# Softmax totals of two attention stages: inverted in their row by VectorE and spread over 64 partitions by one transfer

## The chip, the cores and the metric

The kernel runs on one core of a Trainium2 chip. The metric is the device time of one execution in microseconds (us). Three timed runs of the kernel before gave a median of 3260.16 us (3257.28 to 3265.87). One more execution was profiled; all rows shown here are from that one.

Engines are named as in the profile: PE is TensorE (matmuls), PEld its weight loads, DVE VectorE, ACT ScalarE, POOL GpSimd, SP the engine that only issues transfers.

## The reference

The program is four gated blocks, L0 to L3, each an attention and a feed-forward part, on x of 2 batches x 1024 tokens x 256. The change touches the attentions of L1 (4 heads) and L3 (16 heads); head size is 64, keys are 1024 tokens plus 154 context rows. Cut to what matters, for L3:

```python
dots = jnp.einsum('bhid,bhjd->bhij', q, k) * scale
attn = jax.nn.softmax(dots, axis=-1)
out = jnp.einsum('bhij,bhjd->bhid', attn, v)
return out @ Wo + bo
```

The division of the softmax is done last: a row of ones rides along with v, so that the product gives 64 rows of output and a 65th row with the totals, and the output is multiplied by the inverse of the totals.

## The kernel before, in words

Both stages run the same functions, in **units** of one pair of heads and one batch: L1 has 4 units, L3 has 16. A unit has 40 **slots**; in each, a chunk of up to 128 keys meets a block of 512 queries. Ten slots make one **group** (one head, one block of 512 queries), so a unit has four groups, 0 to 3. In a slot PE multiplies keys with queries (L1978, L1979), ACT takes the exponential (L2022, L2023), in L3 DVE subtracts the rounded high part to get a low part, `pt_lo` (L2129), and PE multiplies with v a few slots later (L1968): `lag` is 4 slots in L3 and 2 in L1, where there is no `pt_lo` and PE takes slots two at a time.

The order on each engine is written out by hand, and each engine works through its list in order. Around the slots a unit also prepares the next one:

- In slots 2 to 11 (L3) PE projects q, k and v of the next unit; ACT rounds them; DVE makes the low parts (L2087, L2075). They go through two side banks in turn, so PE may write a part only when the part two before it was read. In L1 DVE makes low parts in slots 2 to 6 (L2540), and PE's first score waits for all of them (`lo_kept`).
- In slots 8 to 36 PE computes 16 **scores** of the next unit (L1919), one every second slot (two in slots 22, 23 and 24), into one set of three banks. DVE takes the row maximum of each, a `TENSOR_REDUCE` over 1178 columns (L2103). PE may not begin a score before the maximum of the score before it is taken (`maxed`, L1912).
- After the 8th and the 16th score PE transposes the maxima (L1883), in slots 24 and 38, and DVE writes their negatives into the queries (L2066). PE does not begin the next unit before both side banks are read (L1952).
- In slots 14 to 35 PE multiplies scaled outputs with the output weights (L1891) and DVE adds them to x (L2095).

The end of a group runs through four engines. `keep_group` (ACT, L2037) copies 65 rows from the bank into `a.out`, in slot 4 (L3) or 2 (L1) of the next group. SP (`move_totals`) moves the row of totals, 512 numbers in one partition, onto 128 partitions x 4 (`a.totals`, L2138). DVE (`invert_group`) takes the reciprocal there (L2148). SP moves it back into a row (L2141) and waits for it. POOL (`scale_group`) spreads the row over 64 partitions (L2157, a custom instruction) and multiplies (L2161); `ot_done` counts that. ACT waits for `ot_done` of the group two before it ahead of overwriting `a.out`; PE waits for it ahead of the products with the output weights (L1891; for the last unit L1897). DVE inverts a group 7 (L3) or 6 (L1) slots after its end, and group 3 in slot 12 of the next unit. `attention_end` does the last group of the stage. There are 65 inversions in L3 and 17 in L1 (one of each for a dummy group).

The rows of the trace call `a.totals` `l3a_totals` and `l1a_totals`, and so on; in L1 `out_t` is a part of `chip_xn`, and k2 and q2 show as `l3a_k` and `l3a_q`.

Of the kernel before, what the change touches and what calls it, by code (L numbers as in the profile page):

```python
# [19 lines left out]
P = 128  # L20
# [1746 lines left out]
class Attention:  # L1767
# [4 lines left out]
    def __init__(self, sb, psum, sem, projected, gate, split=False, out_t=None):  # L1772
        self.gate, self.split = gate, split
        self.lag = 4 if split else 2
        self.slots_together = 1 if split else 2
        self.pt_slots = 5 if split else 4
        self.exp_slots = 4
        self.prepares = 8 if split else 7
        self.q1 = sb("q1", [P, 2, 2, SEQ], F32R)
        self.q2 = sb("q2", [P, 2, 2, SEQ], F32R)  # L1780
        self.k1 = sb("k1", [P, 2, 2, KEYS], F32R)
        self.k2 = sb("k2", [P, 2, 2, KEYS], F32R)
        self.v = sb("v", [P, 2, KEY_CHUNKS, 2, HEAD + 1], F32R if split else F32)
        self.pt = sb("pt", [P, 4, BLOCK])
        if split:
            self.v_lo = sb("v_lo", [P, 2, KEY_CHUNKS, 2, HEAD + 1], F32R)
            self.pt_hi, self.pt_lo = sb("pt_hi", [P, self.pt_slots, BLOCK], F32R), sb("pt_lo", [P, self.pt_slots, BLOCK], F32R)
            self.v_kept, self.lo_made = sem("v_kept"), sem("lo_made")
        self.maxima = sb("maxima", [P, 16])
        self.minus = sb("minus", [8, 8])  # L1790
        self.out = sb("out", [P, 2, BLOCK])
        self.totals = sb("totals", [P, BLOCK // P])
        self.inverse = sb("inverse", [1, BLOCK])
        self.shared = sb("shared", [P, BLOCK])
        self.out_t = sb("out_t", [P, 2, SEQ]) if out_t is None else out_t
        self.banks = banks = psum("banks", [P, 6, 512])
        self.s_bank, self.st_bank, self.o_bank = banks[:, 0:3, :], banks[:, 3:5, :], banks[:, 5, :]
        self.first_banks = (banks[:, 0:3, :], banks[:, 3:6, :])
        self.side = psum("side", [P, 2, 512])
        self.side_read = [sem("side_read0"), sem("side_read1")]  # L1800
        self.prepared, self.side_done, self.hi_kept = sem("prepared"), sem("side_done"), sem("hi_kept")
        self.q_doubled, self.k_doubled = sem("q_doubled"), sem("k_doubled")
        self.scored, self.maxed, self.st_done, self.exped = sem("scored"), sem("maxed"), sem("st_done"), sem("exped")
        self.pv_done, self.o_kept, self.moved = sem("pv_done"), sem("o_kept"), sem("moved")
        self.inverted, self.returned, self.row_returned = sem("inverted"), sem("returned"), sem("row_returned")
        self.spread_done, self.ot_done, self.passed = sem("spread_done"), sem("ot_done"), sem("passed")
# [326 lines left out]

def move_totals(sp, a, k, g):
    sp.wait_ge(a.o_kept, k + 1)
    sp.dma_start(a.totals[:], a.out[HEAD:HEAD + 1, g % 2, :]).then_inc(a.moved, 16)  # L2138
# [24 lines left out]


# [98 lines left out]
def l1_attention(nc, chip, I):  # L2263
# [7 lines left out]
    with ExitStack() as kept_stack:  # L2271
        sb, _, sem = scope(nc, kept_stack, "l1a")
# [9 lines left out]
        with ExitStack() as stack:  # L2282
            sb, psum, sem = scope(nc, stack, "l1p")
# [216 lines left out]
        with ExitStack() as stack:  # L2500
            sb, psum, sem = scope(nc, stack, "l1a2")
            a = Attention(sb, psum, sem, projected=False, gate=chip.gates[:, 1:2],
                                  out_t=chip.xn[:, 0:8, :].rearrange("p (u t) d -> p u (t d)", u=2))
# [94 lines left out]
def l3_attention(nc, chip, I):  # L2598
# [3 lines left out]
    with ExitStack() as stack:  # L2602
        sb, psum, sem = scope(nc, stack, "l3a")
# [4 lines left out]
        a = Attention(sb, psum, sem, projected=True, gate=chip.gates[:, 3:4], split=True)  # L2608
# [630 lines left out]
```

## Time and profile before

| | us |
|---|---|
| median of three timed runs | 3260.16 |
| the profiled execution: its time | 3260.37 |
| the profiled execution: its span | 3258.7 |
| PE busy in the span | 2897.2 (89%) |
| DVE busy | 1895.9 (58%) |
| ACT busy | 1430.0 (44%) |
| POOL busy | 660.4 (20%) |

The span is from the first to the last instruction; 1.7 us lie around it. Busy shares are means over stages with different limits. L1's attention runs from about 400 to 747 us of the span, L3's from about 1600 to 2862 us. In a timeline a row gives start, duration, engine, line, operation, what it writes from what, and in brackets the idle time ahead of it and what ended it; "issue" means that the profile shows nothing that it waited for.

### The profile page before, as it was taken

How to read it: one execution, taken by the hardware profiler on the slowest of the kernel's cores; microseconds unless marked ns; L12 is line 12 of the kernel's file. 1: busy time of each engine (PE TensorE's matmuls, PEld its weight loads, DVE VectorE, ACT ScalarE, POOL GpSimd, SP SyncE). 2: the span in 40 equal slices, each digit the busy share in tenths (PEclk: the TensorE clock that was granted, in tenths of full speed). 3: DMA queues.
4: the chain of work that ended last, by engine and by line, in shares of the span. 5: the costliest groups of instructions: out<-in, count | busy, mean ns of one | idle time of the engine just before them, and what ended most of it. 6: DMA issues, size and time to landing. Idle time of an engine off the chain costs nothing. (4 is left out here: it accounts for less than half of the span.)

```text
span 3258.7 us, 46897 instructions
## 1 busy us (share of the span) xinstructions
PE 2897.2 (89%) x14020; PEld 2132.3 (65%) x14021; DVE 1895.9 (58%) x3602; ACT 1430.0 (44%) x2987; POOL 660.4 (20%) x736
## 2 busy tenths in 40 slices
PE   6795789975998889999689999999999999579997
PEld 4795455535886679999556666666666666345664
DVE  4414464405555454443588888888888888363333
ACT  1232634431221114544447777767666777321111
POOL 0133101111442200000201111111111111106776
PEclk8797889995999879999789999999999999879999
DMA  1342000002332010000000001010000000035776
GB/s 39 122 148 86 9 20 15 15 1 91 102 103 79 15 40 27 26 13 1 24 21 17 23 15 33 19 23 15 23 21 17 23 15 17 1 70 151 163 163 140
DMA packets 147165, 158.11 MB, mean 49 GB/s; under 512 B 36816, under 2 KB 121702, under 8 KB 146726
## 3 DMA queue, kind: packets, MB, share of 16 engines
q1 hardware_dynamic: 109318, 94.41, 10.5%
q0 software_dynamic: 21280, 37.93, 5.3%
q10 hardware_dynamic: 16416, 24.12, 2.2%
q8 instruction: 50, 0.82, 0.1%
q14 instruction: 101, 0.83, 0.1%
HBM read 105.77 MB, written 29.84 MB: 42 GB/s over the span
## 5 line engine op out<-in xcount | busy, mean ns | idle before, releaser
L2022 ACT ACTIVATE l3a_pt_hi<-l3a_banks 128x512 fp32r<-128x512 f32 (+2 forms) x640 | 382.0, 597 | 322.2 <-PE l3a_banks L1968 255.0
L2129 DVE TENSOR_TENSOR l3a_pt_lo<-l3a_pt,l3a_pt_hi 128x512 fp32r<-128x512 f32 (+2 forms) x640 | 464.0, 730 | 95.5 <-ACT l3a_pt L2023 91.3
L2023 ACT ACTIVATE l3a_pt<-l3a_banks 128x512 f32<-128x512 f32 (+2 forms) x640 | 378.1, 591 | 0.0
L2103 DVE TENSOR_REDUCE l3a_maxima<-l3a_banks 128x1 f32<-128x1178 f32 x256 | 351.1, 1374 | 3.0 <-PE l3a_banks L1919 1.4
L1968 PE MATMUL l3a_banks<-l3a_pt_hi,l3a_v 128*65 128x512 f32 (+2 forms) x640 | 286.4, 447 | 8.1 <-ACT l3a_out L2037 7.3
L1978 PE MATMUL l3a_banks<-l3a_q,l3a_k 128*128 128x512 f32 (+2 forms) x640 | 257.2, 402 | 7.7 <-DVE l3a_q L2066 5.0
L1979 PE MATMUL l3a_banks<-l3a_q,l3a_k 72*128 72x512 f32 (+5 forms) x640 | 254.1, 397 | 0.0
L1968 PE MATMUL l3a_banks<-l3a_pt_hi,l3a_v_lo 128*65 128x512 f32 (+2 forms) x640 | 252.6, 395 | 0.0
L1968 PE MATMUL l3a_banks<-l3a_pt_lo,l3a_v 128*65 128x512 f32 (+2 forms) x640 | 252.6, 395 | 0.0
L1919 PE MATMUL l3a_banks<-l3a_k,l3a_q 128*128 128x512 f32 (+1 forms) x768 | 216.8, 392 | 16.7 <-DVE l3a_maxima L2103 15.4
L2157 POOL PARTITION_BROADCAST l3a_shared<-l3a_inverse x65 | 62.1, 955 | 624.2 <-issue 624.2
L2161 POOL TENSOR_TENSOR l3a_out_t<-l3a_out,l3a_shared 64x512 f32<-64x512 f32 x65 | 88.8, 1366 | 470.5 <-issue 470.5
L1919 PEld LDWEIGHTS l3a_banks<-l3a_k,l3a_q 128*128 128x128 f32 x768 | 142.5, 196 | 62.2 <-DVE l3a_maxima L2103 39.4
L1978 PEld LDWEIGHTS l3a_banks<-l3a_q,l3a_k 128*128 128x128 f32 (+2 forms) x640 | 115.8, 181 | 78.6 <-issue 14.8
L2913 POOL DMA_INDIRECT l3f_sums<-l3f_y_rows,l3f_token_index x96 | 147.8, 1540 | 53.9 <-DVE l3f_row_weight L3176 31.5
L1610 ACT ACTIVATE l2f_hidden_hi<-l2f_p_h,l2f_b_pair 128x512 fp32r<-128x512 f32 x128 | 89.2, 697 | 151.1 <-PE l2f_p_h L1563 140.1
L1968 PE MATMUL l1a_banks<-l1a_pt,l1a_v 128*65 128x512 f32 (+2 forms) x320 | 152.5, 599 | 1.7 <-ACT l1a_out L2037 1.7
L1662 DVE TENSOR_TENSOR l2f_hidden_lo<-l2f_hidden,l2f_hidden_hi 128x512 fp32r<-128x512 f32 x128 | 88.6, 692 | 107.6 <-ACT l2f_hidden L1611 107.6
L1002 PE MATMUL l1f_p_h<-l1f_xt_tile,l1f_w 128*128 128x128 f32 x1184 | 142.3, 279 | 7.1 <-issue 6.1
L1002 PEld LDWEIGHTS l1f_p_h<-l1f_xt_tile,l1f_w 128*128 128x128 f32 x1184 | 138.0, 195 | 14.5 <-issue 14.3
L3009 PE MATMUL l3f_p_h<-l3f_xt,l3f_w 128*128 128x320 f32 x512 | 144.7, 436 | 1.1 <-DVE l3f_xt L3169 1.1
L1577 PE MATMUL l2f_p_y<-l2f_w_hi,l2f_hidden_lo 128*128 128x256 f32 x512 | 144.7, 283 | 0.0
(584 smaller groups left out, 6060.0 us busy)
## 6 DMA issues: line engine op xcount, KB each, us to landing
l3f_w<-in_L_ffn_w SPq DMA_DIRECT2D x96, 256.0 KB, 3.7
l0f_w<-in_L_ffn_W ACTq DMA_DIRECT2D x12, 1024.0 KB, 6.5
l1f_w<-in_L_ffn_W ACTq DMA_DIRECT2D x18, 512.0 KB, 5.1
l2f_w<-in_L_ffn_w SPq DMA_DIRECT2D x16, 512.0 KB, 4.3
l3a_q<-l3a_q SPq DMA_DIRECT2D x64, 128.0 KB, 2.3
l3a_k<-l3a_k SPq DMA_DIRECT2D x64, 128.0 KB, 2.3
l0f_w<-in_L_ffn_W SPq DMA_DIRECT2D x4, 1024.0 KB, 7.2
l1f_w<-in_L_ffn_W SPq DMA_DIRECT2D x6, 512.0 KB, 8.5
```

The costliest lines, as they stand in the source:

```text
L1002: ins = pe.matmul(p_h[:, bank, (f % 2) * P:(f % 2 + 1) * P], w[:, u, c, f * P:(f + 1) * P], xt_tile[:, c * P:(c + 1) * P], start=c == 0, s ...
L1577: ins = pe.matmul(p_y[:, bank, half * D:(half + 1) * D], h[:, n % 2, f, j * P:(j + 1) * P], a[:, u, 1, f * D:(f + 1) * D], start=f == 0 an ...
L1919: ins = pe.matmul(banks[:, c, 0:end - at], lhs, a.k1[:, u, h, at:end], start=True, stop=not masked)
L1968: ins = pe.matmul(a.o_bank[0:HEAD + 1, :], v[0:rows, u, c, h, :], pt[0:rows, slot, :], start=c == 0 and k == 0, stop=c == KEY_CHUNKS - 1 a ...
L1978: pe.matmul(a.st_bank[0:rows, n % 2, :], a.k1[:, u, h, row:row + rows], a.q1[:, u, h, queries], start=True, stop=False)
L1979: pe.matmul(a.st_bank[0:rows, n % 2, :], a.k2[second, u, h, row:row + rows], a.q2[second, u, h, queries], start=False, stop=True).then_inc ...
L2022: act.activation(a.pt_hi[0:rows, n % a.pt_slots, :], a.st_bank[0:rows, n % 2, :], ACT.Exp, bias=bias, scale=scale)
L2023: act.activation(a.pt[0:rows, n % 4, :], a.st_bank[0:rows, n % 2, :], ACT.Exp, bias=bias, scale=scale).then_inc(a.exped, 1)
L2103: dve.tensor_reduce(a.maxima[:, n:n + 1], banks.rearrange("p a b -> p (a b)")[:, 0:KEYS], AX.X, ALU.max).then_inc(a.maxed, 1)
L2129: dve.tensor_tensor(a.pt_lo[0:rows, slot, :], a.pt[0:rows, n % 4, :], a.pt_hi[0:rows, slot, :].bitcast(F32), ALU.subtract).then_inc(a.lo_m ...
L2913: pool.indirect_dma_start(sums, bass.IndirectOffsetOnAxis(token_index[0:n, u, j:j + 1], 0), y_rows[0:n, u, j, :], None, compute_op=ALU.add ...
L3009: ins = pe.matmul(p_h[:, k + f, 0:CAP], w[:, u, c, f * P:(f + 1) * P], xt[:, u, c, :], start=c == 0, stop=c == DC - 1)
```

## The change

`a.totals`, `a.inverse` and the two transfers through them are gone. DVE waits for ACT's copy and takes the reciprocal of the totals in place, in row 64 of `a.out`: 512 numbers in one partition, where it was 4 numbers in each of 128. One transfer, issued by SP, copies that row onto 64 partitions of `a.shared`, which now has two buffers. POOL only multiplies. The inversion stands in slot `lag + 1` of the next group: 5 slots after a group's end in L3, 3 in L1, for group 3 too (slot 5 or 3 of the next unit).

```diff
-        if n == 12:
+        if n == a.lag + 1:
             invert_group(dve, a, number(unit, -1), 3)
-        if n > 10 and n % 10 == (7 if a.split else 6):
+        if n > 10 and n % 10 == a.lag + 1:
             invert_group(dve, a, number(unit, n // 10 - 1), n // 10 - 1)
...
-def move_totals(sp, a, k, g):
-    sp.wait_ge(a.o_kept, k + 1)
-    sp.dma_start(a.totals[:], a.out[HEAD:HEAD + 1, g % 2, :]).then_inc(a.moved, 16)
+def spread_inverse(sp, a, k, g):
+
     sp.wait_ge(a.inverted, k + 1)
-    sp.wait_ge(a.spread_done, k + 1)
-    sp.dma_start(a.inverse[:], a.totals[:]).then_inc(a.returned, 16)
-    sp.wait_ge(a.returned, k * 16 + 16)
-    sp.sem_inc(a.row_returned, 1)
+    sp.dma_start(a.shared[:, g % 2, :], a.out[HEAD:HEAD + 1, g % 2, :].unsqueeze(1).to_broadcast([1, HEAD, BLOCK])).then_inc(a.spread_out[g % 2], 16)
 
 
 def invert_group(dve, a, k, g):
-    dve.wait_ge(a.moved, k * 16 + 16)
-    dve.reciprocal(a.totals[:], a.totals[:]).then_inc(a.inverted, 1)
+
+    dve.wait_ge(a.o_kept, k + 1)
+    totals = a.out[HEAD:HEAD + 1, g % 2, :]
+    dve.reciprocal(totals, totals).then_inc(a.inverted, 1)
...
     pool.wait_ge(a.ot_done, k + 2)
-    pool.wait_ge(a.returned, k * 16 + 16)
     pool.sem_inc(a.passed, 1)
-    pool.partition_broadcast(a.shared[0:HEAD, :], a.inverse[:], channels=HEAD).then_inc(a.spread_done, 1)
-    pool.wait_ge(a.spread_done, k + 2)
-    pool.sem_inc(a.passed, 1)
+    pool.wait_ge(a.spread_out[g % 2], k * 8 + (8 + 8 * (g % 2)))
```

On DVE, in the loop of L3, slots 14 to 16 of a unit before (`l3a_maxima` is the row maximum of a score, `l3a_pt_lo` the slot's low part; REGISTER_ALU and ISA rows are bookkeeping and waits):

```order
L2103 TENSOR_REDUCE l3a_maxima<-l3a_banks 128x1
L2128 REGISTER_ALU
L2129 TENSOR_TENSOR l3a_pt_lo<-l3a_pt,l3a_pt_hi 128x512
L2128 REGISTER_ALU
L2129 TENSOR_TENSOR l3a_pt_lo<-l3a_pt,l3a_pt_hi 128x512
L2094 REGISTER_ALU
L2095 SCALAR_TENSOR_TENSOR chip_x<-l3a_side,chip_gates,chip_x 128x256
L2102 REGISTER_ALU
L2103 TENSOR_REDUCE l3a_maxima<-l3a_banks 128x1
```

The same slots now:

```order
L2101 TENSOR_REDUCE l3a_maxima<-l3a_banks 128x1
L2126 REGISTER_ALU
L2127 TENSOR_TENSOR l3a_pt_lo<-l3a_pt,l3a_pt_hi 128x512
L2142 REGISTER_ALU
L2144 RECIPROCAL l3a_out<-l3a_out 1x512
L2126 REGISTER_ALU
L2127 TENSOR_TENSOR l3a_pt_lo<-l3a_pt,l3a_pt_hi 128x512
L2092 REGISTER_ALU
L2093 SCALAR_TENSOR_TENSOR chip_x<-l3a_side,chip_gates,chip_x 128x256
L2100 REGISTER_ALU
L2101 TENSOR_REDUCE l3a_maxima<-l3a_banks 128x1
```

The reciprocal of group 0 came behind the maximum of slot 16, with 4 columns; it now stands ahead of it, with 512.

On DVE, slots 4 and 5 of a unit in the same loop before (`l3a_k` the low part of the next unit's keys):

```order
L2087 TENSOR_TENSOR l3a_k<-l3a_side,l3a_k 64x512 x2
L2128 REGISTER_ALU
L2129 TENSOR_TENSOR l3a_pt_lo<-l3a_pt,l3a_pt_hi 128x512
L2082 REGISTER_ALU
L2087 TENSOR_TENSOR l3a_k<-l3a_side,l3a_k 64x512 x2
```

And now:

```order
L2085 TENSOR_TENSOR l3a_k<-l3a_side,l3a_k 64x512 x2
L2126 REGISTER_ALU
L2127 TENSOR_TENSOR l3a_pt_lo<-l3a_pt,l3a_pt_hi 128x512
L2142 ISA
L2144 RECIPROCAL l3a_out<-l3a_out 1x512
L2080 REGISTER_ALU
L2085 TENSOR_TENSOR l3a_k<-l3a_side,l3a_k 64x512 x2
```

The reciprocal of the last unit's group 3 has moved here from slot 12, between the two halves of the keys.

On POOL, one group in the same loop before:

```order
L2154 REGISTER_ALU
L2155 ISA
L2157 ISA
L2157 ISA l3a_shared<-l3a_inverse 64x512
L2161 ISA
L2161 TENSOR_TENSOR l3a_out_t<-l3a_out,l3a_shared 64x512
```

And two groups now:

```order
L2152 ISA
L2154 TENSOR_TENSOR l3a_out_t<-l3a_out,l3a_shared 64x512
L2150 REGISTER_ALU
L2152 ISA
L2154 TENSOR_TENSOR l3a_out_t<-l3a_out,l3a_shared 64x512
```

The custom instruction (the ISA row that writes `l3a_shared`) is gone, and with it one ISA row ahead of it and one behind it that had no other line of the program than L2157 and L2161.

## Rows read from the trace of the kernel before

**Rows 1.** Busy us per engine (PE, PEld, DVE, ACT, POOL), granted clock; L3's middle
```profile
1690.00:2760.00 1070.00, 1050.32 (x4759) 726.00 (x4757) 919.32 (x1314) 757.33 (x1518) 137.32 (x118) 1.00 0.09 20
```

**Rows 2.** Single lines: reciprocals on DVE, ns min/median/max, first and last start
```profile
L2148 DVE RECIPROCAL l3a_totals<-l3a_totals x65: 162/169/178, 1685.0 to 2836.5; 128x4 f32<-128x4 f32 x65
...
L3090 DVE RECIPROCAL l3f_total<-l3f_total x1: 253/253/253, 2890.4 to 2890.4; 128x16 f32<-128x16 f32 x1
```

**Rows 3.** Timeline, L3, one unit, slots 15 to 18: DVE, and PE's next score
```profile
2202.47 0.69 DVE L2129 TENSOR_TENSOR l3a_pt_lo<-l3a_pt,l3a_pt_hi 128x512 fp32r<-128x512 f32 x1 [0.35 <-ACT l3a_pt L2023]
...
2203.48 1.37 DVE L2103 TENSOR_REDUCE l3a_maxima<-l3a_banks 128x1 f32<-128x1178 f32 x1
...
2205.78 0.89 PE L1919 MATMUL l3a_banks<-l3a_k,l3a_q 128*128 128x512 f32 x3
```

**Rows 4.** Timeline, the same unit, slots 26 to 28
```profile
2220.98 1.38 DVE L2103 TENSOR_REDUCE l3a_maxima<-l3a_banks 128x1 f32<-128x1178 f32 x1
...
2223.14 0.89 PE L1919 MATMUL l3a_banks<-l3a_k,l3a_q 128*128 128x512 f32 x3
```

**Rows 5.** Timeline, the same unit, slot 38 and PE's start of the next unit
```profile
2239.81 1.21 DVE L2066 TENSOR_TENSOR l3a_q<-l3a_side,l3a_minus 8x1024 fp32r<-8x1024 f32 x1
...
2241.26 0.49 PE L1978 MATMUL l3a_banks<-l3a_q,l3a_k 128*128 128x512 f32 x1 [0.20 <-DVE l3a_q L2066]
```

**Rows 6.** Timeline, the next unit, slot 5 on DVE and slot 7 on PE
```profile
2255.94 1.39 DVE L2087 TENSOR_TENSOR l3a_k<-l3a_side,l3a_k 64x512 fp32r<-64x512 f32 x2 [0.77 <-ACT l3a_k L2057]
...
2257.38 1.16 PE L2635 MATMUL l3a_side<-l3a_w,chip_xt 128*128 128x128 f32 x8
```

**Rows 7.** Timeline, L1, one unit, slots 3 to 8 and 12 to 14
```profile
517.23 1.39 DVE L2540 TENSOR_TENSOR l1a_q<-chip_xt,l1a_q 64x512 fp32r<-64x512 f32 x2 [0.52 <-ACT l1a_q L2521]
...
519.13 4.47 DVE L2540 TENSOR_TENSOR l1a_k<-l1a_k_t,l1a_k 64x512 fp32r<-64x512 f32 x6 [0.52 <-ACT l1a_k L2521]
...
523.65 0.81 PE L1919 MATMUL l1a_banks<-l1a_k,l1a_q 128*128 128x512 f32 x3
...
530.37 0.70 PE L1919 MATMUL l1a_banks<-l1a_k,l1a_q 128*128 128x512 f32 x3
...
531.22 1.38 DVE L2103 TENSOR_REDUCE l1a_maxima<-l1a_banks 128x1 f32<-128x1178 f32 x1 [1.71 <-PE l1a_banks L1921]
...
533.90 0.89 PE L1919 MATMUL l1a_banks<-l1a_k,l1a_q 128*128 128x512 f32 x3
```

**Rows 8.** Transfers by line: issues, KB each, median us to landing
```profile
l3a_q<-l3a_q SPq DMA_DIRECT2D x64, 128.0 KB, 2.3
```

**Rows 9.** Timeline, POOL, one group near the end of L3
```profile
2813.08 0.80 POOL L2157 PARTITION_BROADCAST l3a_shared<-l3a_inverse  x1 [6.14 <-issue]
...
2821.39 1.25 POOL L2161 TENSOR_TENSOR l3a_out_t<-l3a_out,l3a_shared 64x512 f32<-64x512 f32 x1 [7.50 <-issue]
```

**Rows 10.** End of L1: a row of the waits (us, times, longest), then timeline
```profile
PE l1a_side L1897 <- POOL chip_xn L2161: 26.0, 2, 21.6
...
721.05 0.58 ACT L2037 COPY l1a_out<-l1a_banks 65x512 f32<-65x512 f32 x1 [3.45 <-PE l1a_banks L1968]
...
742.57 3.84 PE L1897 MATMUL l1a_side<-l1a_wo,chip_xn 128*128 128x256 f32 x8 [21.55 <-POOL chip_xn L2161]
```

**Rows 11.** L3's last unit and end: two rows of the waits, then timeline
```profile
PE l3a_side L1897 <- issue: 36.0, 2, 23.6
...
PE l3a_banks L1968 <- ACT l3a_out L2037: 7.3, 3, 3.5
...
2833.90 0.58 ACT L2037 COPY l3a_out<-l3a_banks 65x512 f32<-65x512 f32 x1 [2.77 <-PE l3a_banks L1968]
```

**Rows 12.** L3: a wait in another unit, then windows behind it and behind 2775.8
```profile
2434.62 1.07 PE L1919 MATMUL l3a_banks<-l3a_k,l3a_q 128*128 128x512 f32 x3 [1.55 <-DVE l3a_maxima L2103]
...
2434.20:2437.60 3.40, 2.98 (x8) 1.98 (x9) 2.83 (x4) 0.04 (x1) 0.00 (x0) 0.61 0.00 0
...
2775.80:2779.20 3.40, 3.37 (x9) 2.32 (x10) 0.90 (x2) 1.95 (x4) 0.00 (x0) 0.57 0.04 5
```

More of the change, by code:

```diff
@@ L1791, in __init__ @@
         self.out = sb("out", [P, 2, BLOCK])
-        self.totals = sb("totals", [P, BLOCK // P])
-        self.inverse = sb("inverse", [1, BLOCK])
-        self.shared = sb("shared", [P, BLOCK])
+        self.shared = sb("shared", [HEAD, 2, BLOCK])
         self.out_t = sb("out_t", [P, 2, SEQ]) if out_t is None else out_t
@@ L1803, in __init__ @@
         self.scored, self.maxed, self.st_done, self.exped = sem("scored"), sem("maxed"), sem("st_done"), sem("exped")
-        self.pv_done, self.o_kept, self.moved = sem("pv_done"), sem("o_kept"), sem("moved")
-        self.inverted, self.returned, self.row_returned = sem("inverted"), sem("returned"), sem("row_returned")
-        self.spread_done, self.ot_done, self.passed = sem("spread_done"), sem("ot_done"), sem("passed")
+        self.pv_done, self.o_kept = sem("pv_done"), sem("o_kept")
+        self.inverted, self.ot_done, self.passed = sem("inverted"), sem("ot_done"), sem("passed")
+        self.spread_out = [sem("spread_out0"), sem("spread_out1")]
         self.parts = Q_PARTS + V_PARTS if projected else ()
@@ L2130, in attention_dve @@
                               ALU.subtract).then_inc(a.lo_made, 1)
-def move_totals(sp, a, k, g):
-    sp.wait_ge(a.o_kept, k + 1)
-    sp.dma_start(a.totals[:], a.out[HEAD:HEAD + 1, g % 2, :]).then_inc(a.moved, 16)
+def spread_inverse(sp, a, k, g):
     sp.wait_ge(a.inverted, k + 1)
-    sp.wait_ge(a.spread_done, k + 1)
-    sp.dma_start(a.inverse[:], a.totals[:]).then_inc(a.returned, 16)
-    sp.wait_ge(a.returned, k * 16 + 16)
-    sp.sem_inc(a.row_returned, 1)
+    sp.dma_start(a.shared[:, g % 2, :], a.out[HEAD:HEAD + 1, g % 2, :].unsqueeze(1).to_broadcast([1, HEAD, BLOCK])).then_inc(a.spread_out[g % 2], 16)
 def invert_group(dve, a, k, g):
-    dve.wait_ge(a.moved, k * 16 + 16)
-    dve.reciprocal(a.totals[:], a.totals[:]).then_inc(a.inverted, 1)
+    dve.wait_ge(a.o_kept, k + 1)
+    totals = a.out[HEAD:HEAD + 1, g % 2, :]
+    dve.reciprocal(totals, totals).then_inc(a.inverted, 1)
 def scale_group(pool, a, k, g, parity):
     pool.wait_ge(a.ot_done, k + 2)
-    pool.wait_ge(a.returned, k * 16 + 16)
     pool.sem_inc(a.passed, 1)
-    pool.partition_broadcast(a.shared[0:HEAD, :], a.inverse[:], channels=HEAD).then_inc(a.spread_done, 1)
-    pool.wait_ge(a.spread_done, k + 2)
-    pool.sem_inc(a.passed, 1)
+    pool.wait_ge(a.spread_out[g % 2], k * 8 + (8 + 8 * (g % 2)))
     b, (hi, _) = g // 2, head_rows(g % 2)
-    pool.tensor_tensor(a.out_t[hi, parity, b * BLOCK:(b + 1) * BLOCK], a.out[0:HEAD, g % 2, :], a.shared[0:HEAD, :],
+    pool.tensor_tensor(a.out_t[hi, parity, b * BLOCK:(b + 1) * BLOCK], a.out[0:HEAD, g % 2, :], a.shared[:, g % 2, :],
                        ALU.mult).then_inc(a.ot_done, 1)
@@ L2174, in attention_sync @@
         double_parts(sp, a, unit + 1, 1 - u)
-    move_totals(sp, a, number(unit, -1), 3)
-    move_totals(sp, a, number(unit, 0), 0)
+    spread_inverse(sp, a, number(unit, -1), 3)
+    spread_inverse(sp, a, number(unit, 0), 0)
     if extra is not None:
         extra("v4")
-    move_totals(sp, a, number(unit, 1), 1)
+    spread_inverse(sp, a, number(unit, 1), 1)
     if extra is not None:
         extra("o7")
-    move_totals(sp, a, number(unit, 2), 2)
+    spread_inverse(sp, a, number(unit, 2), 2)
 def attention_start_act(act, chip, a):
@@ L2197, in attention_end @@
     if sp is not None:
-        move_totals(sp, a, k, 3)
+        spread_inverse(sp, a, k, 3)
     if dve is not None:
@@ L2583, in _ @@
                 pool.wait_ge(a.prepared, a.prepares)
-                pool.sem_inc(a.spread_done, 1)
                 pool.sem_inc(a.ot_done, 2)
@@ L2739, in _ @@
             pool.wait_ge(a.prepared, a.prepares)
-            pool.sem_inc(a.spread_done, 1)
             pool.sem_inc(a.ot_done, 2)
```

## The prediction

> **What bounds the kernel now.** I read the page first (which engine is busy in which slice), then the windows over the two attentions, then the timeline slot by slot, and the waits at both ends. In the middle of L3 PE is busy 1050.3 of 1070 us at a clock of 1.00, so PE sets the pace; the reader should look at DVE beside it, busy 919.3, or 86% [rows 1]. From the first and the last start of its reciprocals, 64 groups take 1151.5 us, so a unit of four takes 72.0 us [rows 2], and DVE's idle time in it is 14%, 10.1 us. It is not spread so that a long instruction finds room: a gap is such as the 0.35 us in slot 15 [rows 3], and PE's next score waits for DVE's last row maximum. Both stages end otherwise: PE stands still for POOL. At the end of L1 two waits make 26.0 us [rows 10]; in L3's last unit PE waits 36.0 us for the scaled groups and 7.3 us for ACT, which cannot overwrite `a.out` before POOL has read it [rows 11].
>
> **POOL's part.** A group's two POOL instructions take 0.80 and 1.25 us, but 6.1 us lie ahead of the first and 7.5 us ahead of the second, in which POOL waits for nothing that the profile shows [rows 9]. The order shows an extra row ahead of each; they go with the custom instruction. So a group costs POOL 15.7 us before and about 1.3 us after. Within the stage this hides behind PE; at the ends it does not.
>
> **The new reciprocal.** The trace has none with 512 columns. Four columns take 169 ns, 16 take 253 [rows 2]: 7.0 ns for each further column, so 0.169 + 508 x 0.007 = 3.7 us. That 1 partition replaces 128 does not help: a DVE instruction on 8 partitions takes 1.21 us for 1024 columns [rows 5], no less per column than the maximum on 128, 1.37 us for 1178 [rows 3]. From below, 512 columns cannot cost less than a `pt_lo` of 512, 0.69 us [rows 3]; from above, 253 ns for 16 taken as a rate gives 8.1 us. I take the slope. DVE starts an instruction about 0.1 us before the one ahead ends, so it is held for D = 3.6 us.
>
> The Trainium skill, "VectorE: DVE Perf Modes", under "First, the fixed hardware budget", says that the reciprocal divides iteratively, with a repeat count of 8. Eight steps of about 1.04 ns for each of 512 columns would be 4.4 us with a base of 0.1, an estimate by that page; the rows' slope is under seven such steps, and the measured slope decides here.
>
> **What D displaces in L3.** DVE works in order, so everything behind the reciprocal is late by D less the gap it fills.
>
> - Slot 15: the gap of 0.35 is filled, and the maximum of slot 16, which ended at 2204.85, ends D - 0.35 later; PE's score at 2205.78 needs it [rows 3]. PE stands for D - 0.35 - 0.93 = D - 1.3.
> - Slot 25: the maximum that ended at 2222.36 ends D later, the score is due at 2223.14 [rows 4]: D - 0.8.
> - Slot 35: the negated maxima at 2239.81 come D later, less 0.1 for the old reciprocal, and PE opens the next unit 0.2 us after them, waiting already [rows 5]: D - 0.1.
> - Slot 5: the keys' low part comes D - 0.77 late and ended 0.05 us before PE reuses its bank [rows 6]: D - 0.8.
>
> Together 4D - 3.0 = 11.4 us in each of the 15 units that prepare a next one: 171 us. The last unit has no scores; its low parts may be nearly four slots late. Between 0 and 4 x 3.6 us, I take 4.
>
> PE's stops can also cost clock. In one unit the maximum came late, PE stood 1.55 us, and the granted clock over the next 3.4 us was 0.61, most of it 1.2 GHz instead of 2.4; behind the longest wait of the last unit, 3.5 us [rows 11], it was 0.57 [rows 12]. Such a fall costs (1 - 0.6) x 3.4 = 1.4 us. How often it follows a stop two rows cannot tell. I take one fall for three stops: 0.5 us for each of 60, 30 us.
>
> **What D displaces in L1.** DVE has no `pt_lo` here. Slot 3: it takes the place of two gaps of 0.52, and PE's first score begins 0.05 us after the last low part [rows 7]: D - 1.1 = 2.5. Slot 13: it starts as the maximum of slot 12 ends, at 532.5; with 0.4 taken for one addition to x in between and 1.4 for the next maximum DVE is done at 537.9, while a score 3.53 us after that at 533.90 would be due at 537.4: 0.5. Slot 33 likewise; slot 23 stands between two scores of one slot pair, I take 1.5. Three units by 5.0 us: 15 us.
>
> **What the ends give back.** The path after the change is ACT's copy 0.58, reciprocal 3.7, transfer, POOL 1.25 and 0.2 of handing over. The transfer has 64 rows of 2 KB; the q halves are the same size between partitions and land in 2.3 us [rows 8]. That all 64 reads come from one partition no row shows: 2.3 is the lower end, three times it, 6.9, my upper one, which would take 2 x 4.6 = 9 us from the return. That makes 8.0 us from the start of the copy, which begins as PE stops: of L1's 26.0 us of waits 8.1 are left, with PE's next matmul at 729.1 instead of 742.57, and 17.9 come back [rows 10]; in L3 8.1 are left of 36.0 + 7.3, and 35.2 come back [rows 11]. About 3 us more come from falls of the clock that no longer follow the earlier waits, two at 1.4.
>
> **At no cost.** SP issues one transfer for two and no longer waits for one to return; a reader behind it in the queue gains. DVE's new wait for ACT's copy finds it done: the copy stands one slot earlier, and in L3 DVE has already waited for the exponential behind it. If that cover were gone, it is the 0.58 us of the copy.
>
> **Sum**, against the profiled time 3260.4 (the median of the runs shown is 3260.2): + 171 + 4 + 30 (L3) + 15 (L1) - 17.9 - 35.2 - 3 = 3424, rounded 3425 us.
>
> **The rivals.**
>
> - *The idle time takes it (0.16).* If low parts, side banks and scores let DVE run at 100%, only what exceeds its idle time counts: 4 x 3.6 - 10.1 = 4.3 us a unit, 65 in L3, with about 10 in L1 and 56 back: 3280. For it speaks that several buffers lie between the engines; against it that the scores have one set of banks, and PE already waits for a late maximum now and then [rows 12].
> - *The reciprocal is short (0.10), faster.* At 0.69 us, D is 0.6; only slot 35 still delays, 0.5 x 15 = 8, and the ends give 56: 3212. The point that decides is D = 1.6, where slots 5, 15, 25 and 35 cost 0.8, 0.3, 0.8 and 1.5 us, 51 in L3, about what the ends return. Against it stands the slope between 4 and 16 columns; for it, that no row shows 512.
> - *A longer division (0.14).* As a mechanism of these rows: 7.0 ns is a slope between two short instructions, and the shorter may hide part of its steps behind its start, so that the slope is steeper further out, D 4.3 instead of 3.6. Each 0.1 us of D costs 60 x 0.1 in L3 and 12 x 0.1 in L1; 0.7 us more give 50 and 3475. (By the Trainium skill, "VectorE: DVE Perf Modes", the section named above, its estimate is where this rival lies; no row here shows it.)
> - *Every stop costs clock (0.08).* If each of the 60 stops is followed by 3.4 us at half speed, about 1.4 us are lost instead of 0.5, 54 more: 3480. [...]
>
> **Numbers.** The forecast as reckoned has 0.50, its own range 3360 to 3465; 0.02 is left for what I did not think of. The range that should hold 8 in 10 runs from 3275 to 3490: it takes in the longer division, most of the absorbed case and part of the lost clock, and leaves out the short reciprocal. A difference under 0.3%, 10 us, cannot be told from none. Slower holds the forecast, the longer division, the lost clock and most of the absorbed case, 0.86; within 0.3% part of the absorbed case, 0.04; faster 0.10.
>
> **What the new profile would show.** Right: the reciprocal of 1x512 at 3.6 to 4.4 us; in L3's middle units of about 85 us, DVE busy over 90%, PE under 90%, and PE's scores (L1919) waiting for the maxima some 2 to 3 us after slots 15 and 25, and its start of a unit for the negated maxima; POOL with 1.3 us and no gaps of 6 to 7; PE's last wait in each stage about 8 us. Wrong: a reciprocal near 1 us; or a full-length one with units still near 76 us, which means that the buffers took it; or a transfer that lands after 5 us or more.

## The result, and the profile after

The changed kernel takes 3404.67 us (median of 4 runs, 3401.42 to 3411.74), against 3261.28 for the kernel before beside it: a ratio of 1.0442, 95% interval 1.0423 to 1.0462. It is 143 us slower; the prediction was 3425, in a range of 3275 to 3490. The profiled execution took 3411.74 us, 151.4 more than the profiled one of before; the parts below add up to that.

The page and the transfers of the kernel after (busy us, share, instructions; then KB and us from issue to landing):

```profile
PE 2954.8 (87%) x14020; PEld 2155.9 (63%) x14021; DVE 2151.2 (63%) x3602; ACT 1431.8 (42%) x2987; POOL 579.1 (17%) x654
...
L2144 DVE RECIPROCAL l3a_out<-l3a_out 1x512 f32<-1x512 f32 x65 | 217.4, 3344 | 4.7 <-ACT l3a_out L2035 2.7
...
l3a_shared<-l3a_out SPq DMA_DIRECT2D x65, 128.0 KB, 6.3
```

The reciprocal takes 3.34 us and the transfer 6.3. PE has as many instructions as before, but is busy 57.6 us longer: that is clock. One unit in the middle of L3, from the reciprocal of a group 0 to that of the next unit's group 0 (windows, columns as in [rows 1]), first of the kernel before and then of the kernel after:

```profile
2205.36:2278.06 72.70, 71.78 (x328) 49.67 (x327) 64.10 (x92) 51.90 (x105) 9.02 (x9) 1.00 0.08 16
```

```profile
2198.50:2284.00 85.50, 75.52 (x327) 51.14 (x327) 75.11 (x91) 51.63 (x105) 5.13 (x4) 0.96 0.26 28
```

The same work of PE takes 85.5 us. Of the 12.8 us more, 9.1 are idle time of PE (9.98 instead of 0.92) and 3.7 are longer busy time at a clock of 0.96 instead of 1.00. Over 14 units, from one reciprocal of group 3 to the next, a unit takes 85.7 us (1662.48 to 2861.86) and took 73.2 (1684.96 to 2709.52).

PE's waits for DVE in that unit (timeline of PE, kernel after); slot 15's reciprocal started at 2198.47, the others at 2218.93, 2238.51 and 2261.70:

```profile
2204.28 0.81 PE L1917 MATMUL l3a_banks<-l3a_k,l3a_q 128*128 128x512 f32 x3 [1.84 <-DVE l3a_maxima L2101]
...
2212.81 0.81 PE L1917 MATMUL l3a_banks<-l3a_k,l3a_q 128*128 128x512 f32 x3 [0.37 <-DVE l3a_maxima L2101]
...
2215.09 0.80 PE L1917 MATMUL l3a_banks<-l3a_k,l3a_q 128*128 128x512 f32 x3 [0.21 <-DVE l3a_maxima L2101]
...
2224.34 1.35 PE L1917 MATMUL l3a_banks<-l3a_k,l3a_q 128*128 128x512 f32 x3 [2.43 <-DVE l3a_maxima L2101]
...
2243.93 0.27 PE L1881 MATMUL l3a_side<-chip_ident,l3a_maxima 128*8 128x128 f32 x1 [2.34 <-DVE l3a_maxima L2101]
...
2266.52 1.16 PE L2627 MATMUL l3a_side<-l3a_w,chip_xt 128*128 128x128 f32 x8 [2.52 <-DVE l3a_k L2085]
```

Each of the four reciprocals is followed by a stop of 1.8 to 2.5 us. Over the whole run PE waits for DVE in three places more than before (total us, times, longest), first the kernel before:

```profile
PE l3a_banks L1919 <- DVE l3a_maxima L2103: 15.4, 40, 1.6
...
PE l3a_side L1883 <- DVE l3a_maxima L2103: 3.1, 2, 1.6
```

And after, where the wait for the keys' low part has come in with slot 5:

```profile
PE l3a_banks L1917 <- DVE l3a_maxima L2101: 77.6, 73, 2.5
...
PE l3a_side L2627 <- DVE l3a_k L2085: 38.9, 16, 2.5
PE l3a_side L1881 <- DVE l3a_maxima L2101: 38.5, 17, 2.4
```

The granted clock over the 3.4 us behind each stop (windows of PE, kernel after, in the order of slots 15, 25, 35 and 5; PE busy, clock, DMA share, GB/s):

```profile
2204.28:2207.68 3.40, 3.40 (x16) 1.00 0.79 47
2224.34:2227.74 3.40, 3.40 (x9) 0.54 0.77 25
2243.93:2247.33 3.40, 3.40 (x10) 0.59 0.77 27
...
2266.52:2269.92 3.40, 3.40 (x23) 1.00 0.96 31
```

Two of the four are followed by a stretch mostly at 1.2 GHz. The longest stop, that of slot 5, is not, so its length alone does not decide it. Over the 15 units a stretch at the lower clock follows 14 stops of slot 25, 14 of slot 35, 3 of slot 5 and 1 of slot 15: 32 of 60.

The end of L1 in the kernel after (timeline), to be read beside [rows 10]:

```profile
728.30 0.58 ACT L2035 COPY l1a_out<-l1a_banks 65x512 f32<-65x512 f32 x1 [3.46 <-PE l1a_banks L1966]
...
728.91 3.35 DVE L2144 RECIPROCAL l1a_out<-l1a_out 1x512 f32<-1x512 f32 x1 [3.56 <-ACT l1a_out L2035]
...
732.28 0.46 SPq L2137 DMA_DIRECT2D l1a_shared<-l1a_out  x1
...
738.63 1.26 POOL L2154 TENSOR_TENSOR chip_xn<-l1a_out,l1a_shared 64x512 f32<-64x512 f32 x1 [12.53 <-DMA l1a_shared<-l1a_out]
...
740.03 1.19 PE L1895 MATMUL l1a_side<-l1a_wo,chip_xn 128*128 128x256 f32 x2 [11.77 <-POOL chip_xn L2154]
```

One wait of 11.8 us is left of 26.0. The end of L3 looks the same, 11.7 us left of 43.3 [rows 11]. The path is a copy, a reciprocal, a transfer of 6.3 us and a multiplication, and POOL waits for nothing but the transfer.

### The profile page after: what moved, and what is told of

It is laid out like the page before. It is cut to its first block and busy times, and to the rows that moved or that the text cites. A ratio compares the mean times of both kernels' runs of the same rounds, so it can differ in the third digit from the quotient of the medians.

```text
span 3410.0 us, 46109 instructions
## 1 busy us (share of the span) xinstructions
PE 2954.8 (87%) x14020; PEld 2155.9 (63%) x14021; DVE 2151.2 (63%) x3602; ACT 1431.8 (42%) x2987; POOL 579.1 (17%) x654
## 5 line engine op out<-in xcount | busy, mean ns | idle before, releaser
L2127 DVE TENSOR_TENSOR l3a_pt_lo<-l3a_pt,l3a_pt_hi 128x512 fp32r<-128x512 f32 (+2 forms) x640 | 454.6, 722 | 81.1 <-ACT l3a_pt L2021 76.2
L1966 PE MATMUL l3a_banks<-l3a_pt_hi,l3a_v 128*65 128x512 f32 (+2 forms) x640 | 294.9, 461 | 2.4 <-DVE l3a_pt_lo L2127 2.0
L1917 PE MATMUL l3a_banks<-l3a_k,l3a_q 128*128 128x512 f32 (+1 forms) x768 | 221.1, 399 | 78.8 <-DVE l3a_maxima L2101 77.6
L1976 PE MATMUL l3a_banks<-l3a_q,l3a_k 128*128 128x512 f32 (+2 forms) x640 | 265.0, 414 | 3.8 <-DVE l3a_q L2064 2.0
L1977 PE MATMUL l3a_banks<-l3a_q,l3a_k 72*128 72x512 f32 (+5 forms) x640 | 262.9, 411 | 0.0
L1966 PE MATMUL l3a_banks<-l3a_pt_lo,l3a_v 128*65 128x512 f32 (+2 forms) x640 | 261.2, 408 | 0.0
L1966 PE MATMUL l3a_banks<-l3a_pt_hi,l3a_v_lo 128*65 128x512 f32 (+2 forms) x640 | 260.1, 406 | 0.0
L1917 PEld LDWEIGHTS l3a_banks<-l3a_k,l3a_q 128*128 128x128 f32 x768 | 144.1, 201 | 135.6 <-DVE l3a_maxima L2101 114.3
L2144 DVE RECIPROCAL l3a_out<-l3a_out 1x512 f32<-1x512 f32 x65 | 217.4, 3344 | 4.7 <-ACT l3a_out L2035 2.7
L1976 PEld LDWEIGHTS l3a_banks<-l3a_q,l3a_k 128*128 128x128 f32 (+2 forms) x640 | 119.6, 187 | 72.8 <-issue 10.8
```

Of the source, the lines that this page charges most:

```text
L1917: ins = pe.matmul(banks[:, c, 0:end - at], lhs, a.k1[:, u, h, at:end], start=True, stop=not masked)
L1966: ins = pe.matmul(a.o_bank[0:HEAD + 1, :], v[0:rows, u, c, h, :], pt[0:rows, slot, :], start=c == 0 and k == 0, stop=c == KEY_CHUNKS - 1 a ...
L1976: pe.matmul(a.st_bank[0:rows, n % 2, :], a.k1[:, u, h, row:row + rows], a.q1[:, u, h, queries], start=True, stop=False)
L1977: pe.matmul(a.st_bank[0:rows, n % 2, :], a.k2[second, u, h, row:row + rows], a.q2[second, u, h, queries], start=False, stop=True).then_inc ...
L2144: dve.reciprocal(totals, totals).then_inc(a.inverted, 1)
```

## The experiments

The kernel before ran beside each group of runs; ratios are to it. Where totals stay undivided or outputs are zero, the routing of the later feed-forward stages changes a little too (13894 to 14020 matmuls), so stages are compared there, by the first and last start of L3's reciprocals: 1151.5 us apart before [rows 2], 1329.9 after the change.

**1 and 2. How the time goes with the length of the reciprocal.**

```diff
-    totals = a.out[HEAD:HEAD + 1, g % 2, :]
+    totals = a.out[HEAD:HEAD + 1, g % 2, 0:4]              # e1_short
+    totals = a.out[HEAD:HEAD + 1, g % 2, 0:BLOCK // 2]     # e2_half
```

> The changed kernel, but the reciprocal takes only the first 4 of a group's 512 totals (the other 508 stay undivided); transfer, place and POOL's part are those of the change. Theory (the length of the reciprocal on DVE delays row maxima and low parts, and PE stops for them): D falls from 3.3 to about 0.1 us, PE's stops of some 10 us a unit go, only the ends' return is left. Ends: 26.0 and 43.3 us of waits before become about 8.5 each, with 3 of clock: 3261 - 17.5 - 34.8 - 3 = 3206, range 3200 to 3225, faster than the kernel before. Rival (the transfer of one partition's row, 6.3 us and on every unit, is what costs): the transfer is the same, so the time stays at 3390 to 3405. Rival (the earlier slot costs): the slot is the same, 3390 to 3405 too.

> The changed kernel, but the reciprocal takes 256 of the 512 totals (the rest stays undivided). 0.17 + 252 x 0.0062 = 1.74 us. Theory with its four thresholds (stops of D - 0.8, D - 1.3, D - 0.8, D - 0.1 in slots 5, 15, 25, 35): 0.9 + 0.4 + 0.9 + 1.6 = 3.8 us of stops a unit instead of about 10, 57 us in 15 units and some 13 of clock; L1 about 2; ends give back 49 and 3: 3261 + 57 + 13 + 2 - 52 = 3281, range 3260 to 3305. Rival (idle time takes a short instruction up, and only what exceeds DVE's 10 us a unit counts): 4 x 1.74 is under 10, so no stop, 3210 to 3220. Rival (a cost that grows evenly with the columns, without thresholds): midway between the time with 4 columns and the 3405 with 512, about 3305 to 3310.

Four columns: 3212.23 us, ratio 0.985 (0.983 to 0.9871). Half: 3268.31, 1.0021 (1.0008 to 1.0035). The reciprocals of L3 with 4 columns (ns min/median/max, first and last start):

```profile
L2144 DVE RECIPROCAL l3a_out<-l3a_out x65: 168/169/172, 1652.6 to 2802.0; 1x4 f32<-1x4 f32 x65
```

And with half:

```profile
L2144 DVE RECIPROCAL l3a_out<-l3a_out x65: 1743/1744/1746, 1644.7 to 2852.2; 1x256 f32<-1x256 f32 x65
```

First to last start is 1149.4 us with 4 columns, 1207.5 with 256 and 1329.9 with 512. Transfer, slots and POOL's part are the same in all three, so neither the slow transfer nor the earlier slot is the loss: it is the reciprocal's length. The first 256 columns cost 56 us of run time, the next 256 136. So the cost does not grow evenly, as the thresholds of the four stops say, and idle time does not simply take the short one up.

**3. The same division in four pieces.**

```diff
-    dve.reciprocal(totals, totals).then_inc(a.inverted, 1)
+    totals = a.out[HEAD:HEAD + 1, g % 2, piece * P:(piece + 1) * P]
+    ins = dve.reciprocal(totals, totals)      # pieces 0 to 3 in slots lag + 1 to lag + 4
+    if piece == 3:
+        ins.then_inc(a.inverted, 1)
```

> The changed kernel, but each reciprocal of 512 columns is taken as four of 128 columns, about 0.95 us each, in four slots one after the other (slots 5 to 8 of the next group in L3, 3 to 6 in L1); the result is the same. DVE's work rises a little, 4 x 0.95 = 3.8 us a group instead of 3.34. Theory (the length of one hold counts, since gaps and buffers between the engines take a short one): most of the loss goes; DVE's total of some 76 us a unit against 72 is then the bound, 4 to 8 us a unit, 65 to 120 in L3, and 46 come back at the ends: 3280 to 3335. Rival (DVE's total time counts, not the length of a hold): 3405 + 15 x 4 x 0.4 = about 3430, not under 3400.

3387.42 us, 1.0397 (1.0375 to 1.0419): the theory's number failed. PE's waits for DVE (total us, times, longest):

```profile
PE l3a_banks L1917 <- DVE l3a_maxima L2101: 87.6, 102, 1.7
PE l3a_banks L1976 <- DVE l3a_q L2064: 41.6, 16, 2.7
...
PE l3a_side L1881 <- DVE l3a_maxima L2101: 18.2, 17, 1.6
```

No single hold is over 0.95 us, yet the three rows still make 147 us; 77.6, 38.9 and 38.5 make 155 in the changed kernel. What the pieces saved is mostly clock: PE is busy 2926.2 us. The trace of the kernel before tells why there was no gap for them. DVE's idle stretches from the first slot of a unit to slot 37 (timeline of DVE, kernel before; the idle time stands in brackets):

```profile
2171.09 1.00 DVE L2129 TENSOR_TENSOR l3a_pt_lo<-l3a_pt,l3a_pt_hi 128x512 fp32r<-128x512 f32 x1 [2.06 <-ACT l3a_pt L2023]
2173.11 0.69 DVE L2129 TENSOR_TENSOR l3a_pt_lo<-l3a_pt,l3a_pt_hi 128x512 fp32r<-128x512 f32 x1 [1.02 <-ACT l3a_pt L2023]
2175.15 1.39 DVE L2087 TENSOR_TENSOR l3a_q<-l3a_side,l3a_q 64x512 fp32r<-64x512 f32 x2 [1.34 <-ACT l3a_q L2057]
...
2199.15 0.69 DVE L2129 TENSOR_TENSOR l3a_pt_lo<-l3a_pt,l3a_pt_hi 128x512 fp32r<-128x512 f32 x1 [0.34 <-ACT l3a_pt L2023]
...
2226.37 0.69 DVE L2129 TENSOR_TENSOR l3a_pt_lo<-l3a_pt,l3a_pt_hi 76x512 fp32r<-76x512 f32 x1 [0.32 <-ACT l3a_pt L2023]
```

The lines left out hold 1.8 us in slots 3 to 6 and 1.2 in slots 10 and 11, and from 2198 to 2240 there are five more like the last two. So 7.3 of these 9.4 us lie ahead of slot 12, and from there to slot 37, where three of the four reciprocals stand, DVE had 2.05 us. The theory has to say: what counts in such a stretch is DVE's sum, not how long one hold is. In slot 5, where DVE has idle time of its own, the pieces do help: PE's wait there falls from 38.9 to 2.2 us.

**4. The old inversion, without POOL's custom instruction.** The 128x4 reciprocal and its two transfers as before, in the old slots; a third transfer spreads the row over 64 partitions.

```diff
+    sp.wait_ge(a.o_kept, k + 1)
+    sp.dma_start(a.totals[:], a.out[HEAD:HEAD + 1, g % 2, :]).then_inc(a.moved, 16)
     sp.wait_ge(a.inverted, k + 1)
+    sp.dma_start(a.inverse[:, g % 2, :], a.totals[:]).then_inc(a.returned, 16)
+    sp.wait_ge(a.returned, k * 16 + 16)
-    sp.dma_start(a.shared[:, g % 2, :], a.out[HEAD:HEAD + 1, g % 2, :]...
+    sp.dma_start(a.shared[:, g % 2, :], a.inverse[:, g % 2, :]...
```

> The changed kernel with the inversion of the kernel before: the totals go to 128 partitions x 4 by one transfer, the reciprocal of 128x4 stands in the slots of before, the inverses return into a row by a second transfer, and a third spreads the row over 64 partitions, so that POOL has no custom instruction. Theory (the loss is DVE's long reciprocal, the gain is POOL's custom instruction): stages run as in the kernel before, and at an end the path is copy 0.6 + transfer 2.1 + reciprocal 0.2 + transfer 2.1 + spreading transfer 6.3 + POOL 1.3 + 0.4 = 13 us instead of 26.0 in L1 and 43.3 in L3: 3261 - 13 - 30 - 3 = 3215, range 3205 to 3230, faster than both kernels. Rival (three transfers a group in SP's queue collide with the doubling of q and k, or the transfer of 6.3 us delays the last products): no gain, 3250 to 3300.

3228.78 us, 0.9911 (0.9892 to 0.9931), faster than both. The ends came as expected, 12.5 and 12.4 us. That it is not 3215 goes in part with waits that the kernel before has less of (PE waited 1.9 us in all for ACT's `l3a_pt` there):

```profile
PE l3a_banks L1979 <- ACT l3a_pt L2024: 10.5, 11, 1.8
```

and DVE waits 11.4 us for `l3a_totals` instead of 4.6. The rival names three transfers in one queue. Run 9 has three as well, and there these waits are back at 2.9 and 4.6 us: they go with how long the transfers take, the third above all (6.3 us here, 3.5 there), and not with their number.

**5 and 6. The place.**

```diff
+        if n == 12:                                            # e5_late: the slots of before
+        if n > 10 and n % 10 == (7 if a.split else 6):
...
+        if n == (39 if a.split else 33):                       # e6_slot39: group 2 alone
+            invert_group(dve, a, number(unit, 2), 2)
```

> The changed kernel with the reciprocal (512 columns in one partition) back in the slots of before: 7, 7 and 7 slots after a group's end in L3, 6 in L1, and slot 12 for group 3. Theory (DVE's time in a stretch where it has next to none to spare, wherever it stands there): the stops move by two slots, three of four stay as long; slot 12 stands among the first scores and is as bad as slot 5. 3390 to 3420, POOL's last group unmoved. Rival (the earlier slot is what costs): near 3230 to 3300.

> The changed kernel with one of the four reciprocals of an L3 unit moved: that of group 2 goes from slot 35, ahead of the last score's maximum and the negated maxima, to slot 39, behind them, where DVE has its gaps in the trace of before (2.1, 1.0 and 1.3 us in slots 38 to 1). Theory (a reciprocal costs nothing where DVE has idle time of its own): the stops of the transposition of the maxima, 38.5 us over the run, go, and some 8 us of clock with them: 3358, range 3345 to 3375; the other three stay. Rival (DVE's total counts, at whatever place): 3395 to 3410.

The old slots: 3440.7 us, 1.0535 (1.0502 to 1.0569), slower than expected: 36 us more than with the earlier ones. Its waits:

```profile
PE l3a_banks L1917 <- DVE l3a_maxima L2101: 105.9, 87, 2.5
PE l3a_banks L1976 <- DVE l3a_q L2064: 50.9, 16, 3.3
```

Three now stand among the scores, and slot 37's falls whole on the negated maxima (3.3 us a unit). PE is busy 2981.6 us, 27 more than after the change. So the move to earlier slots was a help, not a cost.

Slot 39: 3352.86 us, 1.0277 (1.0251 to 1.0303), as expected; the other two rows of waits stay, and the transposition's is gone:

```profile
PE l3a_banks L1917 <- DVE l3a_maxima L2101: 76.9, 69, 2.5
PE l3a_side L2629 <- DVE l3a_k L2085: 39.0, 16, 2.6
```

A reciprocal in DVE's own idle time adds no stop: 52 us come back, 27 of them as PE's busy time (2927.5).

**7 and 10. Less work for DVE elsewhere, alone and with the pieces.**

```diff
-... banks.rearrange("p a b -> p (a b)")[:, 0:KEYS], AX.X, ALU.max)
+... banks.rearrange("p a b -> p (a b)")[:, 0:KEYS // 2], AX.X, ALU.max)
```

> The changed kernel with each row maximum taken over 589 of the 1178 keys (a softmax is the same with any shift, so the output is too): 0.69 us less for each of 16 maxima, 11 us less DVE work a unit between slots 8 and 38, the reciprocals as they are. If DVE's sum over that stretch counts, the 11 us make up for three reciprocals (10 us): the stops for maxima (77.6 and 38.5 us) nearly vanish and only slot 5's stop, 38.9, stays: 3260 to 3290. If the length of one hold counts, since DVE cannot work ahead of PE's scores, only the one maximum behind each reciprocal is 0.69 shorter: stops of 1.3, 1.8 and 2.4 us stay beside the 2.5 of slot 5, some 37 us and 8 of clock less: 3360, range 3340 to 3375.

> Both edits together: the reciprocal in four pieces of 128 columns in four slots, and each row maximum over 589 keys. Each alone left 3387 and 3295. DVE's work in a unit is then 62 + 15 - 11 = 66 us of 72. If what counts is DVE's sum where it has no time to spare, and, once it has some, how long a single hold is, the two together leave few stops: 3215 to 3245. If the length of a hold plays no part at all, the pieces bring nothing on top: 3290 to 3305.

Alone: 3295.02 us, 1.0101 (1.0077 to 1.0125), far from the 3360 of the hold and just past the range of the sum:

```profile
PE l3a_side L2627 <- DVE l3a_k L2085: 38.5, 16, 2.5
PE l3a_banks L1917 <- DVE l3a_maxima L2101: 28.2, 36, 1.1
PE l3a_side L1881 <- DVE l3a_maxima L2101: 19.0, 17, 1.2
```

The stops for maxima fall from 116 to 47 us, none is over 1.2, and slot 5's is untouched, since no maximum stands ahead of it. Some 14 of the 110 us gained are L1's, which the expectation left out: its attention, whose maxima are halved too, takes 407.6 us from its first matmul to its last and 421.6 in the kernel after. The clock behind slot 5's stop shows that its place does not settle the matter either. Two of its 15 stops of 2.5 us (windows of PE, columns as above):

```profile
1720.90:1724.30 3.40, 3.40 (x23) 1.00 0.96 31
1798.82:1802.22 3.40, 3.40 (x13) 0.54 0.96 31
```

In the kernel after, 3 of 15 were followed by the lower clock; here 9 are, and 9 in run 6 too.

With the pieces too: 3274.91 us, 1.006 (1.0033 to 1.0087), between the two ranges. Slot 5's stop is gone (3.4 us in all), so the length of a hold does play a part there, but the last piece of group 2 stands in slot 38 ahead of the negated maxima, which the expectation overlooked:

```profile
PE l3a_banks L1976 <- DVE l3a_q L2064: 41.6, 16, 2.7
PE l3a_banks L1917 <- DVE l3a_maxima L2101: 24.2, 36, 1.1
```

**8, 11 and 12. The transfer by itself, and POOL's part.**

```diff
-a.out[HEAD:HEAD + 1, g % 2, :].unsqueeze(1).to_broadcast([1, HEAD, BLOCK])
+a.out[0:HEAD, g % 2, :]                                        # e8_probe64, e12_thin64
...
+    pool.tensor_tensor(a.out_t[... first BLOCK // 8 columns], ...)   # e11_thin, e12_thin64
...
+            pool.memset(a.out_t[:], 0.0).then_inc(a.ot_done, 2)      # e11_thin, e12_thin64: once, ahead of L3's units
```

> The changed kernel, but the transfer reads 64 rows of the group's output, one in each of 64 partitions, in place of the one row of inverses 64 times (so the outputs are multiplied by themselves and not by the inverses); bytes, destination and DVE's work are the same. If the reads from one partition make the 6.3 us: it lands in 2.3 us, as the q halves do, each stage's last wait is 4 us shorter, 7.7 instead of 11.7, and the time some 8 us less, about 3397. If the 64 rows written make it: 6.3 again, and no change.

> The changed kernel, but POOL multiplies only 64 of the 512 columns of a group (the rest of L3's scaled output is zero, that of L1 stays as it was): some 0.25 us of POOL a group instead of 1.3. In the changed kernel POOL's multiplication lies beside row maxima that it does not slow down, so this should take off only the 1.0 us at each stage's end: 3400, range 3392 to 3407.

> As the run before it, with the transfer that reads 64 partitions and lands in 2.2 us. Theory (the probe of the transfer gave no time because POOL's multiplication came 5 us earlier, upon a low part that took 1.1 us longer for it, in the stretch where PE waits for DVE): with POOL's part thin the low parts are back at 455 us in total, and the 8 us of the two ends show: 8 us below the run before it, range 4 to 12. Rival (the transfer itself, or other numbers in the data, slow the stage): no gain again, or a loss, with low parts at 490 us.

From 64 partitions the same bytes land in 2.2 us, and each end's wait is 7.7 and 7.6 us. SP's queue moves the same packets and bytes in the kernel after and in the probe; what falls is their time (packets, MB, share of 16 engines' span):

```profile
q1 hardware_dynamic: 92262, 104.82, 18.8%
q1 hardware_dynamic: 92262, 104.82, 11.2%
```

Still its single run took 3410.83 us. POOL's multiplication now comes 4 us sooner after its reciprocal, on top of two low parts (timeline of the probe):

```profile
2203.39 1.28 POOL L2154 TENSOR_TENSOR l3a_out_t<-l3a_out,l3a_shared 64x512 f32<-64x512 f32 x1 [19.91 <-DMA l3a_shared<-l3a_out]
...
2203.42 2.40 DVE L2127 TENSOR_TENSOR l3a_pt_lo<-l3a_pt,l3a_pt_hi 128x512 fp32r<-128x512 f32 x2
```

The two low parts take 2.40 us; at this place in the kernel after they take 1.28, and POOL's 2208.28 falls beside a maximum, which keeps its 1.37. Over L3 the low parts sum to 490.2 us instead of 454.6, and the stops at L1917 to 90.8 instead of 77.6. With POOL's part thin they are 432.9 and 438.8 us, the stops 78.4 and 78.2, and the ends 10.8 against 6.8 us: both as the theory says. In time it was not shown: instead of 4 to 12 us less, 3388.4 (1.0392, 1.0371 to 1.0413) and 3396.28 (1.0399, 1.0376 to 1.0423) cannot be told apart, with 84 matmuls more in the second. The expectation of the first was too high by 12 us; low parts of 433 instead of 455 say that POOL slows some of them in the changed kernel too.

**9. The inverses through device memory.** As the fourth, with the row in device memory.

```diff
-        self.inverse = sb("inverse", [1, 2, BLOCK])
+        row = nc.dram_tensor("l3a_inverse", [1, 2, BLOCK], F32, kind="Internal").ap()   # and one for L1
```

> The kernel with two short transfers, the 128x4 reciprocal and a spreading transfer (e4), with one thing changed: the second transfer writes the inverses to a row in device memory instead of a row in one partition, and the third spreads them from there. If reading one partition 64 times makes the spreading transfer's 6.3 us, it lands in 2.2 to 2.5 us here, each stage's last wait falls from 12.5 to about 9, and the time from 3229 by 7 to 8 us to about 3221, range 3213 to 3228. If the row in device memory is as slow to spread, or its write slower by as much: 3229 and no change.

3210.34 us, 0.9854 (0.9831 to 0.9877): the fastest here of those that invert every total, 48 us under the kernel before it and some 190 under the change. Its transfers:

```profile
l3a_shared<-l3a_inverse SPq DMA_DIRECT2D x65, 128.0 KB, 3.5
...
l3a_inverse<-l3a_totals SPq DMA_DIRECT2D x65, 2.0 KB, 1.4
```

The ends' waits are 9.2 and 9.3 us, as expected, though spreading takes 3.5 us and not 2.2. The profiled executions of the fourth and of this one are 16.9 us apart. Of these 6.4 lie at the ends, 7.3 are shorter busy time of PE (2887.6 instead of 2894.9) for the same number of matmuls, and 3.2 are other waits, where PE's 10.5 for `l3a_pt` fall to 2.9 and some others grow. What makes the busy time shorter no run separates.

## Why the prediction was right, step by step

| step, as the prediction put it | forecast, us | measured, us |
|---|---|---|
| one reciprocal of 512 columns, D | 3.6 | 3.34, and nothing overlaps it |
| stops, slots 15, 25, 35, 5 of a unit | 2.3, 2.8, 3.5, 2.8 | 1.84 and 0.58 behind it, 2.43, 2.34, 2.52 |
| stops in L3's 15 units | 171 | 133.5 (62.2 + 38.9 + 35.4 - 3.0) |
| last unit | 4 | 2.0 |
| clock | 30 - 3 | 57.6 |
| L1's units | 15 | 7.1 |
| given back at the end of L1 | 17.9 | 14.2 |
| given back at the end of L3 | 35.2 | 31.6 |
| sum | +164 | +154.4, of 151.4 |

The measured stops are the rows of PE's waits in the kernel after less those of before: 77.6 less 15.4, 38.9, and 38.5 less 3.1; the wait for the negated maxima falls from 5.0 to 2.0; L1's are 15.5 and 11.2 less 12.7 and 6.9.

- **The mechanism held.** In the middle of L3 the four stops stand where the prediction put them. One had the wrong waiter: slot 35's 2.34 us fall on the transposition of the maxima (L1881), and in the unit shown PE opens the next one without waiting. That DVE's 10 us of idle time would not help was right, but the reason given, gaps too short for a long instruction, was only half of it: short pieces found no room in slots 12 to 37 either (run 3), and a whole reciprocal fits where the idle time lies (run 6). The unit of before was taken at 72.0 us, a mean that takes in the shorter last unit; full units took 73.2. The form 4D - 3.0 gives 4.0 us a unit for 256 columns, and run 2's unit grew by 3.5 (1207.5 less 1151.5, over 16).
- **D was 8% too long.** The slope of 7.0 ns a column came from 4 and 16 columns; from 16 to 512 it is (3344 - 253) / 496 = 6.2. The steeper rival is out. The Trainium skill, "VectorE: DVE Perf Modes", "First, the fixed hardware budget", from whose repeat count of 8 an estimate of 4.4 us was made, does not give the time here.
- **Stops too large, clock too small.** The stops of slots 5 and 25 were 0.3 to 0.4 us shorter than reckoned, mostly as D was, that of slot 35 1.2. The clock fell behind 32 of the 60 stops, not behind one in three, and PE's busy time grew by 57.6 us, 51.6 of them in L3's attention, instead of 27. That the two errors nearly cancel is luck. Which stop costs clock stays open: those of slots 25 and 35, of 2.3 to 2.45 us, were followed by a fall 28 times in 30, and slot 5's, the longest, in 3 of 15 units here and in 9 of 15 in runs 6 and 7.
- **The transfer was mis-sized most.** It was taken at its lower end, 2.3 us, and landed in 6.3, close to the upper one. That is the 4 us missing at each end. It changed nothing else: in the loop it is hidden, as run 1 shows. A transfer that lands after 5 us or more was one of the prediction's own signs of being wrong, and it came; so did a DVE that is busy 88% in the unit shown (75.11 of 85.50 us), where over 90% was expected.
- **L1** cost half of the forecast. Part of it: its keys' low parts, 4.47 us in [rows 7], take 3.48 where POOL does not multiply beside them.
- **The rivals.** A short reciprocal would have been faster, as run 1's 3212 us shows, so the case hung on the length of one instruction. That idle time absorbs it is out by runs 2 and 3.

## What to carry to other kernels

An inversion of one row in one partition is as long as the row: 512 numbers took 3.34 us there, and 0.17 us as 4 columns of 128 partitions. Spread them first, and pay a transfer that is hidden. Before an instruction is lengthened, look at where its engine is idle, not how much: of some 10 us of idle time in a unit only 2 lay in the stretch where the next engine waits and where three of the four reciprocals stood. The good half of this change, a spreading transfer in place of a custom instruction, is worth 48 us when it is taken alone, with the row read from device memory.

## What the runs showed of the hardware

- Reading one partition 64 times is slow: 128 KB land in 6.3 us from one partition and in 2.2 from 64 partitions. The Trainium skill, "SBUF — State Buffer", "Door 1: The DMA port swizzle", gives one port 27.2 GB/s and says that partitions 0 to 63 reach eight: an estimate by that page is 4.8 us against 0.6 for these bytes, 4.2 apart, and the runs show 4.1.
- VectorE's reciprocal of n columns takes 169 ns for 4, 253 for 16, 944 for 128, 1744 for 256 and 3344 for 512, the same on 1 partition (169) as on 128 (169).
- GpSimd's multiplication lengthens a `pt_lo` that it meets by about 1.1 us of its own 1.28, and leaves a row maximum at 1.37. The Trainium skill, "SBUF — State Buffer", "Who interferes with whom", says that a VectorE instruction with two inputs in SBUF contends with GpSimd's reads and that a reduction does not; the traces agree.
- A stop of TensorE of 2.3 to 2.4 us was followed by 3.4 us at a granted clock of 0.54 to 0.59, and one of 2.5 us at another place by 1.00; in run 7 the same 2.5 us were followed by 0.54 in one unit and by 1.00 in another.
